# A transformer block and a gated FFN on eight cores: own slots for the last q tiles, loads and layer norms in another order

## The reference

```python
h = layer_norm(x, ln1_g, ln1_b)                     # x: 4 x 4096 x 1024, float32
q, k, v = h @ wq, h @ wk, h @ wv                    # 4 heads of 256
q = softmax(q * 256**-0.25, over the 256);  k = softmax(k * 256**-0.25, over the 4096 rows)
context = einsum('bhnd,bhne->bhde', k, v);  attn = einsum('bhnd,bhde->bhne', q, context)
a = x + attn @ wo + bo
a = a + gelu(layer_norm(a, ln2_g, ln2_b) @ w_ff1 + b_ff1) @ w_ff2 + b_ff2     # hidden 4096
x = norm(x + a @ w_d + b_d)                         # norm: layer norm without gain
x = norm(x + (silu(x @ w_gate.T / 127) * (x @ w_up.T / 127)) @ w_down.T / 127)  # hidden 3072
```

## Time and profile before

| | |
|---|---|
| median of the runs (lowest, highest) | 1422.54 us (1421.54, 1676.42) |
| profiled execution: time | 1427.1 us |
| its span, slowest core (core 0) | 1425.5 us |
| spans of the eight cores | 1411.5 to 1425.5 us |
| TensorE busy | 1363.9 us, 96% of the span |
| VectorE, ScalarE, GpSimd busy | 551.7, 380.4, 205.5 us |

### The profile page before, as it was taken

The page is one execution under the profiler, slowest core; times in us unless marked ns, Lnnn a source line. Parts: engine busy times, 40 slices in busy tenths (PEclk is TensorE's granted clock), DMA queues, the critical chain, the costliest instruction groups (busy, mean ns, idle before and its releaser), DMA issues.

```text
span 1425.5 us, 17703 instructions; the slowest of 8 cores (1411.5 to 1425.5 us)
## 1 busy us (share of the span) xinstructions
PE 1363.9 (96%) x6484; PEld 628.5 (44%) x6484; DVE 551.7 (39%) x1022; ACT 380.4 (27%) x690; POOL 205.5 (14%) x107
## 2 busy tenths in 40 slices
PE   4899999969997999999999999989999999999997
PEld 3444444425443444444444444434444444444443
DVE  4754555234851122112112555542222222223566
ACT  4423434111671211221221345321111111111224
POOL 4532121205437000000010122200000000000000
PEclk9999999989999999999999999999999999999999
DMA  8654543375935933033010354680020100100112
GB/s 196 170 100 95 118 89 62 50 145 163 173 67 98 183 60 60 0 60 59 1 60 15 84 117 104 159 186 18 0 103 16 60 0 1 59 1 0 60 60 118
DMA packets 104916, 112.95 MB, mean 79 GB/s; under 512 B 90752, under 2 KB 91008, under 8 KB 102144
## 3 DMA queue, kind: packets, MB, share of 16 engines
q1 hardware_dynamic: 101664, 78.00, 21.5%
q0 software_dynamic: 2736, 33.56, 13.1%
q10 hardware_dynamic: 432, 0.27, 0.1%
HBM read 108.66 MB, written 8.39 MB: 82 GB/s over the span
## 4 chain that ended last, share of the span: by engine, by line
PE 88%; DMA 6%; DVE 2%; issue 2%; ACT 1%; POOL 0%; SPq 0%; DVEq 0%; ACTq 0%; POOLq 0%
PE P L933 27%; PE P L1120 21%; PE P L904 14%; PE P L413 9%; PE P L471 6%; PE P L841 4%; PE P L1029 3%; PE P L702 2%; DMA QT<-qn 2%; DMA T<-x3b 1%; DMA xsA<-xkv 1%; DMA S<-wff 1%; PE P L1086 1%; PE P L758 0%; PE P L733 0%
## 5 line engine op out<-in xcount | busy, mean ns | idle before, releaser
L933 PE MATMUL P<-S,GB 128*128 128x512 bf16 x1776 | 391.0, 380 | 9.1 <-DMA S<-wff 9.1
L1120 PE MATMUL P<-T,S 128*128 128x512 bf16 x1408 | 308.5, 381 | 3.8 <-ACT sl L1130 3.8
L940 DVE TENSOR_TENSOR R<-R,P 128x1024 f32<-128x1024 f32 x111 | 135.4, 1220 | 389.8 <-PE P L933 389.8
L933 PEld LDWEIGHTS P<-S,GB 128*128 128x128 bf16 x1776 | 173.9, 98 | 220.1 <-issue 11.5
L904 PE MATMUL P<-T,S 128*128 128x512 bf16 x1024 | 225.1, 379 | 0.2 <-ACT GB L916 0.2
L1120 PEld LDWEIGHTS P<-T,S 128*128 128x128 bf16 x1408 | 138.3, 98 | 172.2 <-issue 7.8
L413 PE MATMUL P<-S,HT 128*128 128x512 bf16 x704 | 159.6, 382 | 3.8 <-ACT HT L328 2.1
L916 ACT ACTIVATE GB<-P,pv 128x512 bf16<-128x512 f32 x128 | 86.0, 685 | 264.1 <-PE P L904 264.1
L904 PEld LDWEIGHTS P<-T,S 128*128 128x128 bf16 x1024 | 100.2, 98 | 121.2 <-issue 0.7
L1130 ACT ACTIVATE sl<-P 128x512 bf16<-128x512 f32 x88 | 52.3, 596 | 361.8 <-PE P L1120 355.8
L1133 DVE SCALAR_TENSOR_TENSOR GB<-sl,P 128x512 bf16<-128x512 bf16 x88 | 60.5, 687 | 215.5 <-PE P L1120 206.9
(11 more groups left out here) (105 smaller groups left out, 855.8 us busy)
## 6 DMA issues: line engine op xcount, KB each, us to landing
S<-wff POOLq DMA_DIRECT2D x8, 2048.0 KB, 16.6
xsA<-xkv SPq DMA_DIRECT2D x16, 512.0 KB, 7.8
xsB<-xkv SPq DMA_DIRECT2D x16, 512.0 KB, 4.5
R<-xkv SPq DMA_DIRECT2D x16, 512.0 KB, 10.7
xsD<-xkv SPq DMA_DIRECT2D x16, 512.0 KB, 4.2
y<-R SPq DMA_DIRECT2D x15, 512.0 KB, 2.6
S<-wgT SPq DMA_DIRECT2D x2, 2048.0 KB, 11.3
S<-wuT SPq DMA_DIRECT2D x2, 2048.0 KB, 10.4
```

Of the source, the lines that this page charges most:

```text
L933: tk = p.pe(lambda e, hc=hc, hf=hf: e.matmul(P[pr][:, hf * 512:(hf + 1) * 512], gb[:, hc * 512 + tile * 128:hc * 512 + tile * 128 + 128], ...
L940: t_R[i] = p.ve(lambda e: e.tensor_tensor(rrow(i), rrow(i), P[pr][:, :], ALU.add), tk, t_R[i])
L1120: tk = p.pe(lambda e, c=c, hc=hc, b=b, sw=sw: e.matmul(bank(b), S[sw][:, c * 1024 + hc * 128:c * 1024 + hc * 128 + 128], T[:, c * 2048 + t ...
```

## The change

Five edits, with the host's arrays to match:

1. `Q_exp` of tiles 28 to 31 writes to four slots of their own in `HT[0]`, which is not used by then, and doesn't wait for earlier transposes.
2. `t_f2[0]`, the first FF2 weights, is issued on GpSimd ahead of all 16 `add_bff2`. The load of that bias moves from behind `turn_h2(15)` to behind `turn_h2(12)`.
3. `t_wn[0]`, the first down weights, is issued after the loop over s and waits for `Y(15)` as well.
4. The first loads form a chain in the order of need. Identity matrix and parameters come in one load. `norm_pool` goes, and `A2` does tiles 0 to 3 too. `T_tile` does tiles up to 11 with the next tile's `A1` inside, and `T_fill` isn't called any more.
5. In steps 8 to 15 the layer norms stand ahead of `G_add`, and `scale_x` stands after `G_pass`, with three quarters of it on ScalarE, not two.

```diff
-    t_qsl = [None, None]
+    t_qsl = [None] * 6
+    def qslot(i):
+        if i < 28:
+            return i % 2, qn[:, (i % 2) * 1024:(i % 2 + 1) * 1024]
+        return i - 26, HT[0][:, (i - 28) * 1024:(i - 27) * 1024]
     def Q_exp(i, pr):
-        s = i % 2
-        q = qn[:, s * 1024:(s + 1) * 1024]
+        s, q = qslot(i)
...
-                accum_out=qs[:, o + 8 + h:o + 9 + h]), t_qm[i], t_qsl[s])
+                accum_out=qs[:, o + 8 + h:o + 9 + h]), t_qm[i], t_qsl[s],
+                t_htfree[0] if i >= 28 else None)
...
+        if i == 12:
+            t_bf2 = p.dma("sync", "bi", BI[:, :], bias_d[128:256, :], t_xb[15])
         if i in (6, 8, 10, 12):
             scale_h2(0, i // 2 - 3, "scalar")
-    t_bf2 = p.dma("sync", "bi", BI[:, :], bias_d[128:256, :], t_xb[15])
...
-    for i in range(4):
-        add_bff2(i)
     t_f2[0] = load_w("gpsimd", 1, f2_d, 0, t_o[15])
-    for i in range(4, 16):
+    for i in range(16):
         add_bff2(i)
...
-        if s == 15:
-            t_wn[0] = load_w("gpsimd", 3, wn_d, 0, t_gbfree[15])
+    t_wn[0] = load_w("gpsimd", 3, wn_d, 0, t_gbfree[15], t_Y[15])
     t_wg[1] = load_w("sync", 4, wg_d, 1, t_W[15])
     t_wu[1] = load_w("sync", 2, wu_d, 1, t_Y[14], t_Y[15], t_W[15])
...
+    load_x(0)
+    load_x(1)
     load_wk(0)
-    load_wk(1)
-    load_x(4, t_wk[0])
-    load_x(5, t_wk[1])
+    load_x(2, t_x[0])
+    load_wk(1, t_x[1])
+    load_x(3, t_wk[0])
+    load_wk(2, t_x[2])
+    load_x(4, t_wk[1])
+    load_wk(3, t_x[3])
+    load_x(5, t_wk[2])
+    load_x(6, t_x[4])
+    load_x(7, t_wk[3])
     A1(0)
+    A2(0)
+    T_tile(0, 1)
+    A2(1)
+    T_tile(1, 2)
     K_quarter(0, 0)
     K_quarter(1, 0)
+    A2(2)
+    T_tile(2, 3)
     K_quarter(0, 1)
+    K_quarter(1, 1)
     K_quarter(2, 0)
+    K_quarter(2, 1)
+    A2(3)
+    T_tile(3, 4)
+    K_quarter(3, 0)
+    K_quarter(3, 1)
+    for i in range(4):
+        K_quarter(i, 2)
     A2(4)
+    T_tile(4, 5)
     for i in range(4):
         K_quarter(i, 3)
         acc_add(i)
...
+        if i < 9:
+            A2(i + 1)
+        if i < 11:
+            T_tile(i + 1, i + 2 if i < 9 else None)
+        if i == 11:
+            A2(15)
+            A1(16)
         K(i, 0 if own else i % 2)
-        if i < 6:
-            T_tile(i + 2)
...
         if g >= 1:
             G_pass(g - 1, c, 2)
+        if last and g >= 1:
+            for f in range(4):
+                unit(u + 1, f)
+        if i == 8:
+            A2(10)
+            A1(11)
+        elif i in (9, 10):
+            for j in (2 * i - 7, 2 * i - 6):
+                A2(j)
+                A1(j + 1)
+        if i >= 11:
+            A(i)
         if g >= 1:
             G_add(g - 1, c, 2)
-        A(i)
```

More of the change, by code:

```diff
@@ L152, in build_nc @@
     bias_d = nc.dram_tensor("bias", [3 * 128, D], F32, kind="ExternalInput")
-    pv_d = nc.dram_tensor("pvec", [128, 194], F32, kind="ExternalInput")
-    cb_d = nc.dram_tensor("cbf", [128, 136], BF16, kind="ExternalInput")
+    pv_d = nc.dram_tensor("pvec", [128, 258], F32, kind="ExternalInput")
     y_d = nc.dram_tensor("y", [NOWN, D], F32, kind="ExternalOutput")
@@ L188, in build_nc @@
     x3b = at("x3b", 2048, BF16, oS2 + 12 * KB)
-    pv = at("pv", 66, F32, oM)
-    cb = at("cb", 136, BF16, oM + 288)
+    pv = at("pv", 130, F32, oM)
+    b1b = at("b1b", 8, BF16, oM + 544)
     ln = at("ln", 192, F32, oM + 576)
@@ L299, in A2 @@
                                                  ALU.subtract, ALU.mult), t, *ring)
-        if 4 <= j < 10:
-            load_x(j + 8)
+        if j < 10:
+            load_x(j + 8, t_x[j + 5] if j < 8 else None)
         elif 16 <= j < 30:
@@ L374, in T_fill, with T_tile @@
         free[b] = t
-    def T_tile(j):
+    def T_tile(j, stats=None):
         u, t4 = j // 4, j % 4
@@ L387, in T_tile @@
                     *([t_xn[j], free[b], t_cb] if k == 0 else []), sig=(k == 3))
+            if stats is not None and hb == (1 if j < 5 else 0):
+                A1(stats)
             for k in range(4):
@@ L391, in T_tile @@
                 dst = ht[:, c * 512 + t4 * 128:c * 512 + t4 * 128 + 128]
-                if hb == 0:
+                if hb == 0 or j >= 8:
                     t = p.se(lambda e, src=src, dst=dst, c=c: e.activation(
-                        dst, src, AF.Identity, bias=pcol(B1, c), scale=pcol(G1, c)), tk, t_pv)
+                        dst, src, AF.Identity, bias=pcol(B1, c), scale=pcol(G1, c)),
+                        tk, t_pv, t_htfree[u % 2])
                 else:
                     t = p.ve(lambda e, src=src, dst=dst, c=c: e.tensor_scalar(
-                        dst, src, pcol(G1, c), pcol(B1, c), ALU.mult, ALU.add), tk, t_pv)
+                        dst, src, pcol(G1, c), pcol(B1, c), ALU.mult, ALU.add),
+                        tk, t_pv, t_htfree[u % 2])
                 t_ht[j][c // 2] = t
@@ L614, in build_nc @@
             t_wq = load_w("gpsimd", 1, wq_d, 0, t_x[15])
-        if last and g == 0:
-            unit(u + 1, 0)
-            unit(u + 1, 1)
+            t_one = p.dma("sync", "ones", ones[:, :], pv_d[:, 130:258])
+        if i < 9:
[5 more added lines that the diff above has]
+            A1(16)
         K(i, 0 if own else i % 2)
-        if i < 6:
-            T_tile(i + 2)
         if own:
@@ L716, in bwv_mm @@
         b = tbank()
+        t_b1 = p.ve(lambda e: e.tensor_copy(b1b[:, :], pv[:, B1:B1 + 8]), t_pv)
         for m in range(8):
             for c in range(8):
-                w = [free[b], t_wv] if m == 0 and c == 0 else []
+                w = [free[b], t_wv, t_b1] if m == 0 and c == 0 else []
                 tk = p.pe(lambda e, m=m, c=c: e.matmul(
@@ L917, in FF1_act @@
                 gb[:, hc * 512:(hc + 1) * 512], bank(b), AF.Gelu,
-                bias=pcol(BF1, q * 8 + hc)), tk, t_gbfree[n - 2] if n >= 2 else t_htfree[n])
+                bias=pcol(BF1, q * 8 + hc)), tk, *([t_gbfree[n - 2]] if n >= 2 else [t_htfree[n]] + t_qsl[2:]))
             free[b] = t_G[n][hc]
@@ L1282, in host_inputs @@
         wgT=wcols(wi("w_gate"), 3), wuT=wcols(wi("w_up"), 3), wdT=wrows(wi("w_down"), 3),
-        bias=np.ascontiguousarray(bias), pvec=pvec, cbf=cbf.astype(BF),
+        bias=np.ascontiguousarray(bias), pvec=pvec,
     )
```

75 lines of the change are left out of this document (12 added, 63 removed).

## The result

The changed kernel takes 1427.17 us (median of 10 executions, lowest 1424.39), the kernel before beside it 1422.51. The ratio is 1.003, with a 95% interval of 1.0018 to 1.0041: no change by the 2% line, and by the interval a little slower. I had predicted 1390.

The account below looks back on a forecast made before the run. TensorE, 96% busy on core 0, was taken as the bound, its waits as the gain. Core 6, then slowest, gains 12.3 + 0 + 13.2 + 7.3 = 32.8 from 1422.54: forecast 1390 us, range 1385 to 1394 (chance 0.44).

Parts of the forecast that it names:

- The adds come 0.6 us later for the issue and some 11 earlier for the bias load that is moved: GpSimd's FF2 bias adds: shifted by the reordered loads, with no cost entered for it.
- Transposes that land with the load [...] leave that add its 10 us: Last stage 2 transposes: landing at 421 to 425 beside the FF2 load, still 10 us ahead of VectorE's add at 436.
- The term itself: FF2 weights: issued at 404.7, landing at 420.4, the wait goes; 10.7 us gained on core 0, 7.3 on core 6.
- my 965 against 968: Down weights: issued at about 947, landing at 965, wanted at 968 when `GU(1)` ends; cost taken as 0.
- rival (d): Down weights come last of three loads, landing at 1004: 36 us of waiting, 2.7 of tail, 1429 us; chance 0.03.
- From there the work is TensorE's: the last quarters 3.45: Start, after the fourth key quarter at 28.2: only TensorE's work left, so `K(8)` starts at 48.0, not 61.26.
- rival (a): Start gains only 5 us, chain links and `T_tile`'s second half waiting; 3 lost at `K(12)`: 1400 us; chance 0.24.
- in one such step of 4 us VectorE has 3.5 us of work: Start, pace per tile: VectorE 3.5 us, ScalarE 3.0, so neither waits for the other for long.
- a bound of 3.5 on the bad side: Stage 1, norms ahead of context sums: sum taken as 0 us, with bounds of -4 and +3.5.
- my wait of 2.4 ahead of `K(12)`: Stage 1: `K(12)` gets a `scale_x` quarter per 1.47 us, takes one per 0.86; 2.4 waiting, tail 1 to 1.8.
- The prediction's own sign of being wrong: DMA engines idle in the first 30 us, or an unlisted wait appearing in stage 1 or at `second(16)`.

Follow-up runs that it names:

- f2_first: The kernel before with the FF2 weight load issued ahead of all 16 bias adds, bias load left in place: median 1415.42 us, ratio 0.9945.
- bias_late: The changed kernel with only the bias load put back behind `turn_h2(15)`: 1400.44 us, ratio 0.9855.
- slots_only: The kernel before with only the four own slots for `Q_exp` of tiles 28 to 31: 1405.75 and 1408.35 us, ratio 0.9893.
- stage1_only: The kernel before with only the new first loads, norms ahead of `G_add` and the new `scale_x` split: 1426.65 us, ratio 1.0041.
- bias_early: The kernel before with only the bias load moved behind `turn_h2(12)`: 1436.47, 1436.55 and 1445.51 us, ratio 1.0131.
- no_acc: `bias_late` without GpSimd's sums of the exponentials of tiles 4 to 27, so its softmax is wrong: 1394.87 us in one execution.
- scale_parity: `bias_late` with `scale_x` split between ScalarE and VectorE as before: 1396.84 to 1412.16 us, ratio 0.9818.
- scale_h2_late: `scale_parity` with ScalarE's four `scale_h2(0, f)` moved behind `attn` of tiles 12 to 15: 1401.72 to 1404.39 us, profiled 1423.17, ratio 0.9847.

## Why the prediction was wrong, step by step

**Edit 2 failed, in a clause that I costed at nothing.** "The adds come 0.6 us later for the issue and some 11 earlier for the bias load that is moved": I took the 11 us for harmless, because GpSimd was idle. They bring the adds from behind `scale_h2` to beside it. The rows were at hand: `scale_h2` over at 416.7 in the kernel before, first add at 416.70. "Transposes that land with the load [...] leave that add its 10 us" looked for lateness in the wrong place. The last two did land late (15.3 and 13.3 us on core 0 after, where the one ahead of the load took 3.1), and in the profiled execution of `f2_first` and in `bias_late` this costs nothing. The term itself was right: the FF2 weights landed at 411.2, the wait of 9.1 went, and `f2_first` holds 28.0 us from `FF1(0)` to the first FF2 block on core 0, where before has 37.3: 9.3 with its tail, against 10.7. What replaced it is +7.2 on core 0 and +25.9 on core 4 (53.9 from `FF1(0)` to the first FF2 block against those 28.0), and the metric takes the worst of eight such cores. I had no rival for it; (c) had VectorE late by 5 for another reason.

**Edit 1 was right.** 13.2 against 13.7 (14.4 in `slots_only`, which has no `b1b` in its way); waits of 0.4 and 1.1 against 0.3 and 1.3.

**Edit 3 was right and worthless.** 6.6 on core 0 against 6.5, nothing on core 4. Alone it doesn't move the metric (1.0006): in the profile of the kernel before only core 0 has that wait, and in those of `stage1_only` and `bias_early` one core each (2.1 and 1.5). The down weights landed at 952.7 and were wanted at 955.7, close to my 965 against 968 less what was gained before; rival (d) is out.

**Edit 4: the loads came as I had them, the work behind them didn't.** The fourth weight load was issued at 19.24 and landed 8.0 later, at 27.2; I had 28.2. `K(8)` started at 53.6 against my 48.0, so 7.6 were gained in place of 13.3 to that point. Two terms failed. The larger is "From there the work is TensorE's: the last quarters 3.45", which puts `K(4)` at 32.2. It started at 35.9, 3.7 later. When the fourth weights landed, TensorE had not only the last quarters before it but most of the block of 44 matmuls at 26.44 as well, tile 3's first two quarters and the third quarters of all four tiles. They stood behind the second half of tile 3's transpose, which VectorE brought only then: tile 4's statistics stood ahead of it, and they waited 1.49 for their x. From 26.4 to `K(4)` TensorE had no gap. That is rival (a)'s mechanism. The smaller is "in one such step of 4 us VectorE has 3.5 us of work": it took 0.81 for a norm, and with 2.3 beside GpSimd's adds it is some 5. The four steps from 35.9 to 53.6 last 3.9, 4.4, 4.8 and 4.7, together 1.9 more than my 15.8. `no_acc`, without the later two of these adds, has 0.81 for the norm and 1.0 less for the four steps, so the adds are a reason. They aren't the only one: the last step waits 0.59 for ScalarE, which does both halves of tile 8.

**Edit 5: 0, with a bound of 3.5 on the bad side, was too kind.** Stage 1 gave back all 7.6. I read the split of `scale_x` the wrong way round, so my wait of 2.4 ahead of `K(12)` (2.95 measured) had the right size for a wrong reason, and I had none ahead of `K(20)` and `K(24)`, which cost 6.1. The old split gives 5.9 back (`scale_parity`), and no adds give 6.8 (`no_acc`). I haven't run both together, so how far these overlap is open. The 1.1 for `b1b` was in no term. The prediction's own sign of being wrong, a wait in stage 1 that its list hadn't, came with `K(20)` and `K(24)`.

**The sum.** With the bias load late the kernel is at 1400.4, where rival (a), less from the start, had 1400. The number matches by luck: (a) had 5 gained at the start, where 7.6 were, and 3 lost at `K(12)`, where `K(12)`, `K(20)`, `K(24)` and a `G_pass` lost 12.4 against the 3.9 of before. Of the 37 us between 1390 and 1427 25 to 27 are the bias load, and the rest is mostly stage 1.

## What to carry to other kernels

Before an operation of GpSimd is moved, lay the time it will cover over VectorE's list: if VectorE then has operations like the two that grew here (`scale_h2` and the norm to bf16), both may take turns (2.43 us for 0.41), and at worst one VectorE operation waits for almost GpSimd's whole run (34.6 us). A load that looks late may be what keeps two engines apart. When a change is the same on eight cores and the metric is the slowest, a loss that can fall on any core counts in full, and a gain counts only if all have it.

## What the runs showed of the hardware

Not every operation of VectorE suffers beside GpSimd's float32 adds. Core 0 of `bias_late`, during the adds:
```profile
412.81 27.99 POOL L956 TENSOR_TENSOR R<-R,BI 128x1024 f32<-128x1024 f32 x12 [19.97 <-DMA BI<-bias]
...
423.36 1.22 DVE L941 TENSOR_TENSOR R<-R,P 128x1024 f32<-128x1024 f32 x1 [3.23 <-PE P L934]
```
An add with an operand from PSUM keeps its 1.22 us, and the layer norm's statistics keep their 0.68 (they read float32 and write six numbers). The bf16 `scale_h2` goes from 0.41 to 2.43 and the norm to bf16 from 0.81 to 2.3. The Trainium skill (SBUF — State Buffer, SBUF: two separate sides) has the lock for VectorE's fast modes, and for its operations with two operands from SBUF beside a GpSimd operation that reads SBUF. The two that keep their time read one operand there, which agrees; in which mode any of the four ran no run shows. Who is served is not regular: turns on core 0 and six others, and one operation left standing for 34.6 us on core 4, in the same execution of the same program; in `bias_early` one is left standing for 28.2 us on all eight cores. What decides that stays open.

The time of a DMA transpose beside a weight load scatters as much: 3.1 us, 13 to 22, and 38 to 43 on core 3 of `scale_parity` and core 7 of `scale_h2_late`, where the loads themselves took 38.1 and 42.3. It lands with the load or as if alone, and which of them changes from core to core.
